# A scan over states on five engines: ScalarE waits for another count of transposes before it fills the first turned buffer of the next unit

## The reference, cut to what matters

```
def step(h, inp):
    x_t, dt_t, B_t, C_t = inp
    dA = jnp.exp(dt_t[:, :, None] * A[None])
    h = dA * h + (dt_t * x_t)[:, :, None] * B_t[:, None, :]
    y = jnp.einsum('bdn,bn->bd', h, C_t) + D * x_t
    return (h, y)
```

## Time and profile before

| what | value |
|---|---|
| three runs | 4217.56, 4224.65, 4225.96 us, median 4224.65 |
| span of the profiled execution, first to last instruction | 4222.2 us |
| scan stage in it, first scan to last | 257.9 to 1946.2 us |
| mean granted PE clock over the span | 0.909 |
| busy over the span | PE 81%, DVE 66%, ACT 58%, POOL 45% |

### The profile page before, as it was taken

The page is one execution under the profiler, slowest core; times in us unless marked ns, Lnnn a source line. Parts: engine busy times, 40 slices in busy tenths (PEclk is TensorE's granted clock), DMA queues, the critical chain, the costliest instruction groups (busy, mean ns, idle before and its releaser), DMA issues. The chain is left out here.

```text
span 4222.2 us, 69815 instructions
## 1 busy us (share of the span) xinstructions
PE 3401.3 (81%) x22940; PEld 2121.0 (50%) x22940; DVE 2787.7 (66%) x4369; ACT 2464.7 (58%) x3860; POOL 1886.3 (45%) x1761
## 2 busy tenths in 40 slices
PE   8567878878788787885876999999999976599980
PEld 4146666666666666664553333333333335366660
DVE  3258888888888888886764777777777727100105
ACT  3268888888888888884220555665566552122110
POOL 1048888888888888885541000010001015200006
PEclk9679999999999999998995999999999996799995
DMA  6533333333333333334634001011001025122205
GB/s 204 156 101 91 91 91 91 91 91 91 92 91 89 93 91 89 91 93 183 236 119 120 9 19 19 7 19 22 17 9 19 9 64 189 34 83 83 83 31 188
DMA packets 158040, 357.64 MB, mean 85 GB/s; under 512 B 20931, under 2 KB 65974, under 8 KB 143216
## 3 DMA queue, kind: packets, MB, share of 16 engines
q1 hardware_dynamic: 125392, 266.42, 22.8%
q0 software_dynamic: 16784, 52.10, 3.5%
q10 hardware_dynamic: 15504, 34.61, 2.2%
HBM read 253.24 MB, written 102.26 MB: 84 GB/s over the span
## 5 line engine op out<-in xcount | busy, mean ns | idle before, releaser
L506 POOL TENSOR_TENSOR scan_hC<-scan_hh,scan_cbc 128x512 f32<-128x512 f32 x1024 | 1382.8, 1379 | 160.1 <-DVE scan_hh L718 101.4
L718 DVE TENSOR_TENSOR_SCAN scan_hh<-scan_dA,scan_state,scan_bx 128x512 f32<-128x512 f32 x1024 | 1252.4, 1264 | 213.9 <-PE scan_bx L810 99.5
L810 PE MATMUL scan_bx<-kept_ident,scan_dBxT 128*128 128x128 f32 x4096 | 677.3, 292 | 197.5 <-DVE scan_hh L718 133.5
L1561 PE MATMUL attend_s<-attend_kt,attend_qt 32*128 32x512 f32 (+3 forms) x2560 | 793.7, 609 | 33.9 <-DMA attend_qt<-attend_zero 27.6
L559 ACT ACTIVATE scan_dBxT<-scan_dtxT,scan_bt 128x512 f32<-128x512 f32 x1028 | 655.7, 711 | 81.6 <-PE scan_bx L810 81.4
L820 PE MATMUL scan_acc<-kept_ident,scan_hC 128*128 128x128 f32 x4128 | 656.8, 287 | 56.1 <-ACT scan_uu L568 29.3
L810 PEld LDWEIGHTS scan_bx<-kept_ident,scan_dBxT 128*128 128x128 f32 x4096 | 502.4, 150 | 389.7 <-DVE scan_hh L718 232.1
L554 ACT ACTIVATE scan_dA<-scan_dt,scan_an 128x512 f32<-128x512 f32 x1028 | 660.9, 712 | 29.1 <-DVE scan_hh L718 29.1
L1582 PE MATMUL attend_s<-attend_qt,attend_kt 32*128 32x512 f32 (+3 forms) x2560 | 635.7, 581 | 17.9 <-POOL attend_pb L1438 14.6
L1472 DVE TENSOR_REDUCE attend_mx<-attend_s 128x1 f32<-128x512 f32 x768 | 494.5, 686 | 197.0 <-PE attend_s L1561 195.8
L1532 ACT ACTIVATE attend_pb<-attend_s 128x1024 f32<-128x1024 f32 x384 | 390.8, 1024 | 279.1 <-PE attend_s L1582 279.1
(11 more groups left out here) (207 smaller groups left out, 3675.1 us busy)
## 6 DMA issues: line engine op xcount, KB each, us to landing
scan_xs<-scratch_xin SPq DMA_DIRECT2D x288, 256.0 KB, 6.2
scan_cbc<-scratch_crows SPq DMA_DIRECT2D x64, 1024.0 KB, 4.8
scratch_y<-scan_uu ACTq DMA_DIRECT2D x17, 1024.0 KB
scratch_xin<-proj_out_x SPq DMA_DIRECT2D x8, 1024.0 KB
scratch_sz<-proj_out_z SPq DMA_DIRECT2D x8, 1024.0 KB
scratch_exp_in<-proj_cleared SPq DMA_DIRECT2D x8, 1024.0 KB, 8.4
mix_yf<-scratch_y SPq DMA_DIRECT2D x8, 1024.0 KB, 6.6
mix_yb<-scratch_y SPq DMA_DIRECT2D x8, 1024.0 KB, 9.5
```

Of the source, the lines that this page charges most:

```text
L506: pool.tensor_tensor(hC[n % 2][:, m, :], h[:, m, :], rows, ALU.mult).then_inc(hc_ok, 1)
L718: dve.tensor_tensor_scan(hh[n % 2][:, m, r], dA[n % 2][:, m, r], bx[bank(j)][:, r], state[:, d, n, m:m + 1], ALU.mult, ALU.add).then_inc(h ...
L810: last = pe.transpose(bx[bank(j)][:, t * P:(t + 1) * P], dBxT[turned_slot(n)][:, t, m * P:(m + 1) * P], k["ident"][:, :])
L1561: pe.matmul(s1[v % S1][:, 0:w], qt[n % SETS][rows, t * P:(t + 1) * P], kt_[n % SETS][rows, c * C:c * C + w], start=True, stop=True).then_i ...
```

## The change

The wait of ACT ahead of the spread in iteration 15 gets another count.

```
                     if n + 1 == NS:
                         act.wait_ge(fr_out, first + FR_TURN + JT)
-                    act.wait_ge(bx_mm, f * SUB + turned_free(n + 1 if n + 1 < NS else NS))
+                    if n + 1 < NS:
+                        act.wait_ge(bx_mm, f * SUB + turned_free(n + 1))
+                    else:
+                        act.wait_ge(bx_mm, f * SUB + SUB + turned_free(0))
                     spread_b(dn, at)
```

## The result

The changed kernel takes 4152.68 us (median of four runs, 4148.46 to 4158.22) against 4223.45 us for the kernel before, a ratio of 0.9833 with a 95% interval of 0.9819 to 0.9847: 71 us faster. The forecast was 4156.

A forecast was written before the change was run, and what follows sets the result against it. No engine fills the period; ACT leads from unit end to scan 18. Fourteen ends at 4.72 us (66.1) plus about 2.4 at the loop's turn make 68.5 us: from median 4224.65 to 4156 us, range 4147 to 4176.

The forecast's parts named there:

- The wait removed, and whether it comes back: At each unit end, ACT's spread 0 starts 4.72 us earlier; new wait at spread 1 priced at 0, at most 0.1.
- the clock: PE's granted clock in units: mix unchanged; as bounds, 2.2 us more won, or 0.35 us a unit, 5 us, lost.
- What follows on DVE, POOL and PE: From unit end to scan 18: DVE gains 2.54 to 3.29 us, waits supply the rest; all engines 4.72 us earlier.
- The loop's turn: Where the loop turns, PE and scan 0 don't move, add 0 was held 1.51 us; gain about 2.4 us.
- DVE's gain is all there is: Rival: scans 12 to 18 wait for something else, only DVE's 3.29 us count: 49 us, 4175 us; chance 0.10.
- POOL leads: Rival: POOL, without a pause in a unit's last third, gains only 2.5 us: 38 us, 4187 us; chance 0.04.
- the wait only moves: Rival: ACT stands in front of spread 1 as long as before spread 0: nothing changes, 4225 us; chance 0.04.
- Slower, by PE's clock: Rival: PE's lower rate from evacuation to `bt_out` eats the gain; wholly low, 3.9 us a unit, 4283 us; chance 0.04.

## Why the prediction was right

*The wait removed, and whether it comes back.* 4.72 us at a unit end were to go and nothing to come in front of spread 1. Both are in the rows. Without the period of the turn, 14 periods went from (1587.23 - 105.66) / 14 = 105.83 to (1518.11 - 102.62) / 14 = 101.11 us: 4.72 us each, the term as priced. (That it fits to the hundredth is in part luck; see the clock, below.)

*What follows on DVE, POOL and PE.* At scan 18 DVE is 4.72 us earlier, as forecast, but the way there differs in part. DVE gained its 3.29 us at the end. The rest came ahead of scan 12: the 20 scans take 23.53 us, where in four pieces they took 9.47 + 1.28 + 1.28 + 12.30 = 24.33, and the wait of 1.21 us became 0.41. Scans 15 and 18 wait 1.04 and 1.78 us as before; I had counted their waits among those that DVE makes up. So PE too was ready for the evacuation 4.0 us earlier, and kept 0.82 of its 1.59 us in front of it; I had it arrive with 0.1 to spare if DVE won all 3.29 us. Inject 0 at the full rate is part of that. POOL still waits 0.62 of its 3.28 us in front of the adds, so it doesn't lead either.

One reading of mine was wrong: DVE did not lose 3.29 us at each unit end. That holds for ends like the earlier trace rows, behind which PE runs at its lower rate. At others it does not, such as the one at 569.06 us in the kernel before, where inject 0 takes 0.65 us:

```profile
572.75 9.61 DVE L718 TENSOR_TENSOR_SCAN scan_hh<-scan_dA,scan_state,scan_bx 128x512 f32<-128x512 f32 x8 [2.09 <-PE scan_bx L810]
...
589.96 3.80 DVE L718 TENSOR_TENSOR_SCAN scan_hh<-scan_dA,scan_state,scan_bx 128x512 f32<-128x512 f32 x3 [2.34 <-PE scan_bx L810]
...
600.49 1.28 DVE L718 TENSOR_TENSOR_SCAN scan_hh<-scan_dA,scan_state,scan_bx 128x512 f32<-128x512 f32 x1 [1.77 <-ACT scan_dA L554]
```

DVE loses 2.09 us at this end, waits longer ahead of scan 12, and scan 18 comes 600.49 - 569.06 = 31.43 us behind spread 0 all the same. This is one more place where DVE's delay vanishes while ACT's 4.72 us stay. The extra work on DVE and late on ACT, both hidden, and the extra work early on ACT, paid in full, show that ACT leads here, and that the time is not a coincidence of sums.

*The loop's turn* was priced at 2.4 us and gave 105.66 - 102.62 = 3.04; 2.60 of it are there by scan 18, which comes 33.54 us behind spread 0 instead of 31.42, and the rest comes behind it. Its rows in the changed kernel, in order of time:

```profile
1065.50 0.83 PE L813 MATMUL scan_bx<-kept_ident,scan_dBxT 128*128 128x128 f32 x4 [2.90 <-ACT scan_dBxT L559]
...
1067.20 0.20 POOL L490 MEMSET scan_state<- 128x128 f32 x1 [0.78 <-issue]
...
1067.87 17.68 DVE L721 TENSOR_TENSOR_SCAN scan_hh<-scan_dA,scan_state,scan_bx 128x512 f32<-128x512 f32 x15 [4.07 <-POOL scan_state L490]
...
1090.92 1.28 DVE L721 TENSOR_TENSOR_SCAN scan_hh<-scan_dA,scan_state,scan_bx 128x512 f32<-128x512 f32 x1 [0.80 <-PE scan_bx L813]
```

Scan 0 waits for POOL to clear the state. For PE the list names ACT, but spread 0 had ended by 1059.93 us, so it is the turn itself, as the row of before had it. ACT then waits 4.3 us for the last adds, the one wait that the change did create.

*The clock* was the term sized wrongly. I allowed 0.35 us a unit, from the 0.3 by which units of before differ. In the changed kernel they differ by 0.9: beside the turn, five take 100.5 to 100.6 us, seven 101.4 to 101.5, and two 101.2. A unit at the high clock gained 105.67 - 100.62 = 5.05 us and one at the low clock 105.98 - 101.40 = 4.58, so that the mean came out at 4.72 only by the numbers in which they come. That is luck, of some tenths of a us in a unit.

*The rivals.* "DVE's gain is all there is" and "POOL leads" fall by the time itself (4175 and 4187 us) and by the early extra work on ACT, which would have been hidden; "the wait only moves" falls by spread 1. "Slower, by PE's clock" did not happen, but its mechanism is real: with half of the wait removed it took 0.66 us of the unit shown.

By the Trainium skill ("TensorE: Matmul & The Clock Gate", Part 1), which says that activity releases the throttled rate, I had put 2.2 us more. At the unit ends the trace agrees: inject 0 now runs at the full rate. But little time was to be had there: in the kernel before the unit from 674.73 us, whose granted clock was 0.50 from 675.8 to 682.5, lasted 105.73 us, and the one from 569.06, which had no such stretch at its start, 105.67. Over the whole unit there is little change: the mean clocks of the periods lay between 0.92 and 0.97 before and lie between 0.93 and 0.97 now, and the low stretches sit elsewhere.

## What to carry to other kernels

Where engines are all busy for nine tenths of a period, ask of each wait whether the engine that stands there leads on from it: follow it down until another engine's wait for it has nothing to spare, and look for a place where a delay of the other engine vanished. A semaphore's count that asks for a later event than the buffer's last user costs the time that the engine stands in front of it, if that engine leads: here 4.72 us, though the event that was needed lay twelve tiles further back. And two edits that each give little can give much together, when the one moves a wait into what the other removes.

## What the runs showed that I had not expected

PE's granted clock reaches the period by way of a buffer. In the changed kernel a slow unit has PE at its lower rate ahead of scan 49 (in order of time):

```profile
436.12 1.06 PE L813 MATMUL scan_bx<-kept_ident,scan_dBxT 128*128 128x128 f32 x4
...
437.31 1.28 DVE L721 TENSOR_TENSOR_SCAN scan_hh<-scan_dA,scan_state,scan_bx 128x512 f32<-128x512 f32 x1 [0.88 <-PE scan_bx L813]
...
437.81 0.60 PE L813 MATMUL scan_bx<-kept_ident,scan_dBxT 128*128 128x128 f32 x4
...
446.63 2.56 ACT L559 ACTIVATE scan_dBxT<-scan_dtxT,scan_bt 128x512 f32<-128x512 f32 x4 [1.06 <-PE scan_bx L813]
```

DVE is held 0.88 us, and through the four copies and turns behind it inject 55 comes late, and so does spread 15, 1.06 us; in quick units such as the one that ends at 754 us ACT waits 0.2 us or less there. The kernel before paid for a delay at this place too, since its spread 0 hung on inject 63, and that on scan 61: in each of its units the next spread 0 came 0.75 us behind the end of scan 61. But there PE's slow stretch was shorter. These are two windows of granted clock 0.50, the first in the changed kernel's unit from 350.05 us, the second in the unit from 569.06 of the kernel before (columns as in the earlier trace rows), and then DVE's wait for scan 49 in that second unit:

```profile
431.00:437.60 6.60, 5.80 (x27) 5.80 (x28) 5.72 (x6) 4.73 (x7) 6.60 (x7) 0.50 0.00 0
...
651.90:655.20 3.30, 3.13 (x16) 3.16 (x16) 3.30 (x4) 2.33 (x4) 3.30 (x5) 0.50 0.00 0
```

```profile
655.66 1.28 DVE L718 TENSOR_TENSOR_SCAN scan_hh<-scan_dA,scan_state,scan_bx 128x512 f32<-128x512 f32 x1 [0.23 <-PE scan_bx L810]
```

The first stretch lasts to 87.6 us behind spread 0 and covers the inject of scan 49; the second lasts to 86.1, and DVE is held 0.23 us. Why the slow stretches lie and last otherwise in the changed kernel was not tried. With a fourth buffer spread 15 doesn't ask for inject 55, and units with a clock of 0.93 and of 0.98 take the same 100.3 us.
